# Shared experts of the second FFN in fp32r parts, dummy matmuls in TensorE's waits, and a pair of additions moved ahead of the row maximum

## The chip, the cores and the metric

The kernel runs on one core of a Trainium2 chip. Its time is the device time of one execution in microseconds; a figure for a kernel is the median of its runs. The engines are TensorE (PE in the profile, with its weight loads as PEld), VectorE (DVE), ScalarE (ACT), GpSimd (POOL) and SyncE (SP, which only issues DMAs).

## The reference

Two blocks, each an attention and a mixture of experts with gated residuals, on x of 4 x 512 x 256 in fp32 (2048 tokens):

```python
x = x + tanh(g_xattn[0]) * sliding_window_attention(layernorm(x), ctx, ctx)   # 16 heads, window 64
x = x + tanh(g_ffn[0]) * moe0(layernorm(x))      # 32 experts, 8 per token, 1 shared expert
x = x + tanh(g_xattn[1]) * coattention(layernorm(x), ctx)
x = x + tanh(g_ffn[1]) * moe1(layernorm(x))      # 8 experts, 2 per token, 2 shared ones
# coattention(enc, ctx):
Sim = (enc @ w1)[:, :, None] + (ctx @ w2)[:, None, :] + einsum('bid,bjd->bij', enc * w3, ctx) + b
hq  = softmax(Sim, axis=2) @ ctx
bar = softmax(max(Sim, axis=2), axis=1) @ enc    # one row per batch
out = concatenate([enc, hq, enc * hq, enc * bar]) @ W_qv + b_qv
# the shared experts of moe1:
z = (silu(xt @ sw1.T) * (xt @ sw3.T)) @ sw2.T    # 256 -> 512 -> 256
```

## The kernel before

Tokens lie in 16 tiles of 128 rows, four tiles to a batch (TPB = 4). The 256 columns are two halves of 128 (CH = 2). Each engine has its own instruction list, written out by hand in the order in which it is to run; semaphores tie the lists together. The program runs in these stages (microseconds of the profiled execution): the window attention, 0 to 251; `front0_tensor` with the routing of the first FFN, 256 to 343; its sparse loop over 159 blocks, 347 to 611; its shared expert and the first gathers of its result, 612 to 659; the coattention in four rounds, one for each batch, with the shared experts of the second FFN in between, 671 to 903; the rest of that FFN's routing, to 936; its sparse loop, 939 to 1081; the last shared part and the stores.

`front0_tensor` transposes the normalised rows (L767), forms the logits (L821), counts the mask's ranks (`ranks`, L787) once VectorE has chosen the experts, and builds the list of tokens by slot (`table`, L801: for each of 16 tiles eight matmuls of a one-hot `hot_tok` and a one-hot `hot_hi`, both read with a step of eight elements). `expert_row` follows, and then the sparse loop's first gather.

Stage two, round b. TensorE runs, as its list is written: `transposes(b)` (L1472), `scores(b)` (L1485), `inputs_turned(b-1)` and `logits(b-1)` of the batch before (L1558, L1569), `shared_gate_up(b-1, 0)` (L1585), `probs_transposed(b)` (L1497), `maxima_transposed` (L1503), `attended(b)` (L1520, between its halves `maximum_spread`, L1507, which waits for VectorE's `nmx`), `shared_gate_up(b-1, 1)`, `context_bar(b)` (L1529), `shared_gate_up(b-1, 2)`, half of `output(b)` (L1545), `shared_gate_up(b-1, 3)`, the other half. `shared_down(b-2)` (L1632) stands between the transposes and the scores of rounds 2 and 3, `shared_down(2)` behind round 3, and `shared_down(3)` behind the second sparse loop. A unit u of the shared experts is 128 of the 512 hidden columns: `shared_gate_up` is 2 x CH fp32 matmuls of 512 columns, ScalarE takes the silu (L1680), VectorE multiplies (`shared_hidden`, L1803, into `hid`), and `shared_down` is 4 x 4 fp32 matmuls of 256 columns. Their weights, `wsh1`, come with one DMA that SP issues in round 1.

VectorE adds the first FFN's expert rows to x in pairs of tiles (`y_pair_added`, L1193, 16 additions), two pairs for each batch; POOL gathers these rows (`yg`, L1178) as ring slots come free. In round b VectorE adds the pairs of batch b+1 and then normalises them (L720 to L751 into `xn`), which `transposes(b+1)` waits for. In round b >= 2 `shared_added(b-2)` (L1640) stands ahead of `logits_taken` (L1796).

## Time and profile before

| | us |
|---|---|
| runs | 1104.25, 1104.73, 1109.32 |
| median | 1104.73 |
| profiled execution | 1107.14 |
| its span, first to last instruction | 1105.3 |
| TensorE busy | 904.4 (82%) |
| VectorE busy | 696.2 (63%) |
| ScalarE busy | 441.5 (40%) |
| POOL busy | 538.2 (49%) |
| mean granted TensorE clock | 0.894 of full |

The shares are averages over stages that differ: in the sparse loops TensorE is busy nearly always, in routing it waits for VectorE. The granted clock takes two values, 1.0 (2.4 GHz) and 0.5 (1.2 GHz); a value between them is a mean over a stretch that has both. The same matmul lasts twice as long at 0.5.

### The profile page before, as it was taken

The numbers are of one execution on the slowest core, as the hardware profiler recorded it, in microseconds if no ns is written. First come the engines' busy times: TensorE is split into PE (matmuls) and PEld (weight loads), VectorE is DVE, ScalarE is ACT, GpSimd is POOL, SyncE is SP. The second block draws the span as 40 slices with busy tenths as digits, with TensorE's granted clock in tenths as the row PEclk, the third lists the DMA queues.
The fourth block names the chain that finished last, engine by engine and source line by source line (L and its number), as shares of the span: only waits on it lengthen the run. The fifth ranks groups of instructions, "written<-read, shape, count | busy, mean of one in ns | idle before, by whom it ended". The sixth has DMA issues, their size and how long they took to land.

```text
span 1105.3 us, 20321 instructions
## 1 busy us (share of the span) xinstructions
PE 904.4 (82%) x5372; PEld 692.5 (63%) x5373; DVE 696.2 (63%) x2004; ACT 441.5 (40%) x1030; POOL 538.2 (49%) x575
## 2 busy tenths in 40 slices
PE   3468888887297999999999904879999996998893
PEld 2357777777144888888888502545656563787672
DVE  6669999996664865555555256765868246443334
ACT  4558888992051444444444302122322313232220
POOL 7246656644004755555552577874700000687641
PEclk9679999995556999999999966969999998899997
DMA  8860000003101777777768738342300011466647
GB/s 248 212 123 3 1 0 0 0 1 107 43 1 51 220 219 202 224 215 220 214 192 138 281 95 278 105 141 80 112 6 20 1 61 23 82 111 127 139 75 243
DMA packets 75225, 127.42 MB, mean 115 GB/s; under 512 B 12481, under 2 KB 52033, under 8 KB 75009
## 3 DMA queue, kind: packets, MB, share of 16 engines
q0 software_dynamic: 21264, 48.02, 19.5%
q1 hardware_dynamic: 32240, 57.47, 17.1%
q10 hardware_dynamic: 21632, 20.85, 5.4%
q8 instruction: 44, 0.72, 0.3%
q14 instruction: 45, 0.36, 0.1%
HBM read 80.62 MB, written 36.77 MB: 106 GB/s over the span
## 4 chain that ended last, share of the span: by engine, by line
PE 60%; DVE 19%; issue 6%; DMA 6%; POOL 3%; ACT 2%; SPq 2%; DVEq 0%; ACTq 0%; POOLq 0%
PE bank L899 18%; PE bank L914 9%; PE bank L1585 5%; PE bank L888 4%; DVE ptl L609 4%; PE bank L801 3%; DMA sw<-in_w 3%; POOL yg L1178 3%; PE bank L1485 3%; DVE nmax L601 2%; PE bank L907 2%; PE bank L419 2%; DVE x L1193 2%; PE bank L1520 2%; PE bank L1632 2%
## 5 line engine op out<-in xcount | busy, mean ns | idle before, releaser
L1163 POOL DMA_INDIRECT xg<-token_rows,gather_idx x198 | 190.7, 963 | 318.3 <-DMA token_rows<-cw 135.6
L899 PE MATMUL bank<-sw,xgt 128*128 x948 | 247.5, 384 | 0.0
L899 PEld LDWEIGHTS bank<-sw,xgt 128*128 128x128 f32 x948 | 167.6, 193 | 15.2
L1178 POOL DMA_INDIRECT yg<-slot_rows,slot_of x128 | 137.0, 1070 | 70.3 <-issue 33.5
L992 ACT ACTIVATE ssil<-bank 128x128 f32<-128x128 f32 x237 | 65.7, 278 | 202.1 <-PE bank L899 202.1
L914 PE MATMUL bank<-sw,sht 128*128 x474 | 145.0, 388 | 0.0
L1084 DVE COPY xgt<-bank 128x256 f32<-128x256 f32 x198 | 83.9, 424 | 85.4 <-PE bank L888 77.3
L1097 DVE COPY sht<-bank 128x128 f32<-128x128 f32 x237 | 69.1, 291 | 106.4 <-PE bank L907 106.1
L537 ACT ACTIVATE prob<-bank,nmax 128x256 f32<-128x256 f32 x256 | 111.7, 511 | 7.5 <-DVE nmax L601 7.5
L419 PE MATMUL bank<-consts,prob 128*128 128x128 f32 x512 | 83.5, 288 | 34.7 <-DVE ptl L609 32.2
L601 DVE TENSOR_REDUCE nmax<-bank 128x2 f32<-128x512 f32 x128 | 87.6, 685 | 16.6 <-PE bank L406 15.7
L888 PE MATMUL bank<-consts,xg 128*128 128x128 f32 x396 | 78.2, 280 | 19.2 <-DMA xg<-token_rows,gather_idx 10.9
L527 ACT ACTIVATE pth<-bank 128x512 f16<-128x512 f32 x128 | 80.1, 626 | 31.9 <-PE bank L419 31.7
L419 PEld LDWEIGHTS bank<-consts,prob 128*128 128x128 f32 x512 | 57.4, 145 | 49.9 <-ACT prob L537 28.1
L609 DVE TENSOR_TENSOR ptl<-bank,pth 128x512 f16<-128x512 f32 x128 | 87.0, 680 | 1.1 <-ACT pth L527 0.8
L914 PEld LDWEIGHTS bank<-sw,sht 128*128 128x128 f32 x474 | 71.6, 191 | 19.7 <-issue 1.8
L888 PEld LDWEIGHTS bank<-consts,xg 128*128 128x128 f32 x396 | 56.0, 144 | 41.7 <-DMA xg<-token_rows,gather_idx 13.0
L1142 POOL DMA_INDIRECT token_sums<-ysb,scatter_idx x39 | 61.8, 1584 | 35.5 <-ACT ysb L999 31.8
L1007 ACT ACTIVATE ysb<-bank 128x256 f32<-128x256 f32 x159 | 61.1, 384 | 44.0 <-PE bank L914 43.5
L653 POOL TENSOR_TENSOR qm<-qst,consts 128x512 fp32r<-128x512 f32 x64 | 67.6, 1087 | 21.9 <-ACT qst L469 21.9
L406 PE MATMUL bank<-kst,qm 128*128 (+1 forms) x256 | 77.6, 386 | 0.0
L1090 DVE TENSOR_TENSOR shid<-ssil,bank 128x128 f32<-128x128 f32 x237 | 66.2, 280 | 4.7 <-ACT ssil L992 4.5
(216 smaller groups left out, 1570.5 us busy)
## 6 DMA issues: line engine op xcount, KB each, us to landing
slot_rows<-ysb ACTq DMA_DIRECT2D x79, 256.0 KB, 3.4
sw<-in_w SPq DMA_DIRECT2D x48, 384.0 KB, 3.6
kst<-khl SPq DMA_DIRECT2D x32, 224.0 KB, 5.6
token_sums<-zeros SPq DMA_DIRECT2D x2, 2176.0 KB, 12.1
token_rows<-xn SPq DMA_DIRECT2D x8, 512.0 KB, 3.6
sums<-token_sums SPq DMA_DIRECT2D x8, 512.0 KB, 7.2
xg<-token_rows,gather_idx POOLq DMA_INDIRECT x198, 3.5
x<-in_x SPq DMA_DIRECT2D x4, 512.0 KB, 6.7
```

The lines of the kernel that those rows point to most:

```text
L406: mm = pe.matmul(sp[:, hh * WIN:(hh + 1) * WIN], qm[:, par, hh, k, :], ks, start=False, stop=True, skip_group_check=True)
L419: mm = pe.transpose(bank[2 + (k + 1) % 2][:, hh * WIN + kb * P:hh * WIN + kb * P + P], prob[:, (k + 1) % 4, hh, kb * P:(kb + 1) * P], ident)
L527: nc.scalar.activation(pth[:, (k + 1) % 4], bank[2 + (k + 1) % 2][:, :].rearrange("p (a b) -> p a b", a=2), ACT.Copy).then_inc(s_pth, 1)
L537: e = nc.scalar.activation(prob[:, k % 4, hh, :], s_bank(k, par)[:, hh * WIN:(hh + 1) * WIN], ACT.Exp, bias=nmax[:, k % 4, hh:hh + 1])
L601: nc.vector.tensor_reduce(nmax[:, k % 4, :], s_bank(k, par)[:, :].rearrange("p (a b) -> p a b", a=2), AX_X, ALU.max, negate=True).then_inc ...
L609: nc.vector.tensor_tensor(ptl[:, k % 4], bank[2 + k % 2][:, :].rearrange("p (a b) -> p a b", a=2), pth[:, k % 4], ALU.subtract).then_inc(s ...
L888: mm = pe.transpose(bank[i % 2][:, c * P:(c + 1) * P], xg[:, (first + i) % XG_RING, c * P:(c + 1) * P], ident)
L899: mm = pe.matmul(bank[2 + k % 2][:, 0:2 * FF], xgt[:, i % 3, c * P:(c + 1) * P], w[:, :, c, :], start=(c == 0), stop=(c == CH - 1))
L914: pe.matmul(bank[6 + i % 2][:, 0:DIM], sht[:, k % 2, :], sw[:, bass.ds(slot[i] + u, 1), 2 * CH * FF:WCOLS], start=(u == 0), stop=(u == hal ...
L1084: nc.vector.tensor_copy(xgt[:, i % 3, :], bank[i % 2][:, 0:CH * P]).then_inc(s_xtl, 1)
L1163: nc.gpsimd.indirect_dma_start(xg[:, (first + i) % XG_RING, 0:ROW[L]], None, rows[L], bass.IndirectOffsetOnAxis(gather_idx[:, i:i + 1], 0) ...
L1178: nc.gpsimd.indirect_dma_start(yg[:, t % Y_TILES, j, :], None, ybuf[L], bass.IndirectOffsetOnAxis(slot_of[:, t, j:j + 1], 0)).then_inc(s_y ...
```

## The change

Three things change.

First, the second FFN's shared experts. Each fp32 operand is replaced by a high part, rounded to fp32r by a ScalarE copy, and a low part, the rest, by a subtract: `whi`/`wlo` for the weights (copied by ScalarE and subtracted by VectorE once, ahead of round 0), `xh`/`xl` for the inputs of each batch (`inputs_high` on ScalarE, `inputs_low` on VectorE), `hh`/`hl` for the hidden values (`hidden_high` on ScalarE; `hidden_low` on VectorE for batches 0 and 3, on POOL for 1 and 2). Each fp32 matmul becomes three fp32r ones: high x high, low x high, high x low. The raw weights now come by two DMAs (1 MB and 0.5 MB) that SP issues as soon as the first sparse loop is through, into `prob1` and `hq`, which are free there. TensorE gets waits for `wlo`, `xlo` and `hlo`.

Second, `kept_busy`: n matmuls of the identity with 256 fp32 columns of constants into a bank whose content is not used. They stand behind the window attention (4 and 5), ahead of and behind the ranks (7, 5), ahead of the table (8, behind a wait for VectorE's 21st routing step, the slots' positions), behind both `expert_row` (8, 8), ahead of the first transposes of stage two (7), behind the scores of rounds 0 and 1 (7, 5) and behind the outputs of round 0 (8).

Third, `y_pair_added(0, 4b+4)`, the first pair of the next batch, moves on VectorE from behind `negated_maximum(b)` to ahead of `shared_hidden(b-1, 0)` and `largest(b)`.

```diff
-        wsh1 = sb("wsh1", [P, SH1, WCOLS], F32)
+        whi = sb("whi", [P, SH1, WCOLS], F32R)
+        wlo = sb("wlo", [P, SH1, WCOLS], F32R)
...
+        def kept_busy(pe, to, n):
+
+            for _ in range(n):
+                pe.matmul(to[:, 0:DIM], ident, consts[:, 0:DIM], start=True, stop=True)
...
-            for k in range(5):
+            for k in range(4):
                 step(TILES, k, 0, True)
+            pe.wait_ge(s_p, UNITS)
+            kept_busy(pe, bank[4], 4)
+            step(TILES, 4, 0, True)
+            kept_busy(pe, bank[4], 5)
...
             logits(3)
+            pe.wait_ge(m.rs, 5)
+            kept_busy(pe, bank[7], 7)
             ranks(pe, 0, m)
+            kept_busy(pe, bank[7], 5)
+            pe.wait_ge(m.rs, 21)
+            kept_busy(pe, bank[7], 8)
             table(pe, 0, m, range(TILES))
             expert_row(pe, 0, m)
+            kept_busy(pe, bank[7], 8)
...
+                if L == 1 and 2 <= k < 2 + 2 * SH1 and k % 2 == 0:
+                    hidden_high(act, m, BATCH - 1, (k - 2) // 2)
...
+                if L == 1 and 6 <= k < 6 + 2 * SH1 and k % 2 == 0:
+                    hidden_low(dve, nc.vector, BATCH - 1, (k - 6) // 2)
...
                 if b == 1:
-                    sp.dma_start(wsh1[:, :, :], w1_in[0:SH1].rearrange("u p c -> p u c")).then_inc(m.wload, 16)
...
                 if v == 0:
-                    pe.wait_ge(m.wload, 16)
+                    pe.wait_ge(A["wlo"], SH1)
                 else:
                     pe.wait_ge(m.h, n1["h"] + v)
                 if u == 0:
                     pe.wait_ge(A["p"], 4 * min(b + 2, BATCH))
+                    pe.wait_ge(A["xlo"], CH * (b + 1))
                 for half, ready in ((0, m.gate), (1, m.up)):
+                    n = 0
                     for c in range(CH):
                         w = slice((CH * half + c) * FF, (CH * half + c + 1) * FF)
-                        mm = pe.matmul(bank[half][:, :], wsh1[:, u, w], xt[:, 0, c, :], start=(c == 0), stop=(c == CH - 1))
+                        for wp, xp in ((whi, xh), (whi, xl), (wlo, xh)):
+                            mm = pe.matmul(bank[half][:, :], wp[:, u, w], xp[:, c, :], start=(n == 0), stop=(n == 5))
+                            n += 1
                     mm.then_inc(ready, 1)
             pe.wait_ge(A["par"], 64)
             pe.wait_ge(A["wq"], 16)
+            pe.wait_ge(moe[0].acc, BATCH)
+            pe.wait_ge(s_yadd, 4 * TOP0 - 4)
+            kept_busy(pe, bank[7], 7)
             pe.wait_ge(A["one"], 1)
...
                 scores(b)
+                if b == 0:
+                    kept_busy(pe, bank[7], 7)
+                if b == 1:
+                    kept_busy(pe, bank[7], 5)
...
                     shared_gate_up(b - 1, 3)
                 output(b, (2,))
+                if b == 0:
+                    kept_busy(pe, bank[7], 8)
...
         def shared_down(pe, m, b):
-            pe.wait_ge(m.h, m.n["h"] + SH1 * (b + 1))
+            pe.wait_ge(A["hlo"], SH1 * (b + 1))
...
             for j in range(TPB):
+                n = 0
                 for u in range(SH1):
-                    mm = pe.matmul(bank[6 + j // 2][:, (j % 2) * DIM:(j % 2 + 1) * DIM], hid1[:, u, j * P:(j + 1) * P],
-                                   wsh1[:, u, 2 * CH * FF:WCOLS], start=(u == 0), stop=(u == SH1 - 1))
+                    for hp, wp in ((hh, whi), (hh, wlo), (hl, whi)):
+                        mm = pe.matmul(bank[6 + j // 2][:, (j % 2) * DIM:(j % 2 + 1) * DIM], hp[:, u, j * P:(j + 1) * P],
+                                       wp[:, u, 2 * CH * FF:WCOLS], start=(n == 0), stop=(n == 3 * SH1 - 1))
+                        n += 1
...
+        def hidden_high(act, m, b, u):
+            act.wait_ge(m.h, m.n["h"] + SH1 * b + u + 1)
+            nc.scalar.activation(hh[:, u, :], hid1[:, u, :], ACT.Copy).then_inc(A["hhi"], 1)
+
+        def hidden_low(eng, ops, b, u):
+            eng.wait_ge(A["hhi"], SH1 * b + u + 1)
+            ops.tensor_tensor(hl[:, u, :], hid1[:, u, :], f32(hh[:, u, :]), ALU.subtract).then_inc(A["hlo"], 1)
...
+                if b == 0:
+                    act.wait_ge(A["wlo"], SH1)
...
+            def inputs_high(b):
+                if b:
+                    act.wait_ge(m.up, m.n["up"] + SH1 * b)
+                for c in range(CH):
+                    act.wait_ge(m.xh, m.n["xh"] + 2 * b + c + 1)
+                    nc.scalar.activation(xh[:, c, :], xt[:, 0, c, :], ACT.Copy).then_inc(A["xhi"], 1)
+
+            act.wait_ge(m.wload, 32)
+            for part, source in ((gate_up_cols, prob1), (down_cols, down_raw)):
+                for u in range(0, SH1, 2):
+                    nc.scalar.activation(whi[:, u:u + 2, part], source[:, u:u + 2, :], ACT.Copy).then_inc(A["whi"], 1)
...
                 softmax(b)
                 if b:
                     inputs_copied(b - 1)
+                    inputs_high(b - 1)
                     shared_silu(b - 1, 0)
                 probs_copied(b)
                 row_exp(b)
                 attended_copied(b)
                 if b:
                     for u in range(1, SH1):
+                        hidden_high(act, m, b - 1, u - 1)
                         shared_silu(b - 1, u)
+                    hidden_high(act, m, b - 1, SH1 - 1)
...
+            def inputs_low(b):
+                for c in range(CH):
+                    dve.wait_ge(A["xhi"], CH * b + c + 1)
+                    nc.vector.tensor_tensor(xl[:, c, :], xt[:, 0, c, :], f32(xh[:, c, :]), ALU.subtract).then_inc(A["xlo"], 1)
+
             y_pair_added(dve, 0, 0)
+            n = 0
+            for part, source in ((gate_up_cols, prob1), (down_cols, down_raw)):
+                for u in range(0, SH1, 2):
+                    n += 1
+                    dve.wait_ge(A["whi"], n)
+                    nc.vector.tensor_tensor(wlo[:, u:u + 2, part], source[:, u:u + 2, :], f32(whi[:, u:u + 2, part]),
+                                            ALU.subtract).then_inc(A["wlo"], 1)
             y_pair_added(dve, 0, 2)
...
                 encoder(b)
+                if b == 2:
+                    hidden_low(dve, nc.vector, 0, 3)
                 if b:
                     residual(b - 1)
...
                 if b >= 2:
                     shared_added(dve, m, b - 2)
                 if b:
+                    inputs_low(b - 1)
                     logits_taken(b - 1)
+                if b + 1 < BATCH:
+                    y_pair_added(dve, 0, 4 * b + 4)
+                if b:
                     shared_hidden(b - 1, 0)
                 largest(b)
                 negated_maximum(b)
-                if b + 1 < BATCH:
-                    y_pair_added(dve, 0, 4 * b + 4)
+                if b == 1:
+                    hidden_low(dve, nc.vector, 0, 0)
                 products(b)
                 if b:
                     shared_hidden(b - 1, 1)
                 row_softmax(b)
                 weights_by_bar(b)
+                if b == 1:
+                    hidden_low(dve, nc.vector, 0, 1)
                 if b:
                     shared_hidden(b - 1, 2)
                 if b + 1 < BATCH:
                     y_pair_added(dve, 0, 4 * b + 6)
+                    if b == 1:
+                        hidden_low(dve, nc.vector, 0, 2)
...
             for t in range(TILES):
                 y_gathered(pool, 0, t)
+            for b in (1, 2):
+                for u in range(SH1):
+                    hidden_low(pool, nc.gpsimd, b, u)
...
             sp.wait_ge(s_sye, BLOCKS[0])
+            raw = w1_in[0:SH1].rearrange("u p c -> p u c")
+            sp.dma_start(prob1[:, :, :], raw[:, :, 0:2 * CH * FF]).then_inc(moe[1].wload, 16)
+            sp.dma_start(down_raw, raw[:, :, 2 * CH * FF:WCOLS]).then_inc(moe[1].wload, 16)
             parameters_a1(sp)
```

On VectorE in round 0, before, between the last normalised probabilities (`prob`) and the second pair; `nmx` is the row maximum, `ngmx` its spread form, `w` the weights of the context bar:

```order
L1730 TENSOR_SCALAR prob<-prob,rd 128x512
L1744 TENSOR_REDUCE nmx<-bank 1x1
L1748 COPY ngmx<-bank 128x1
L1193 SCALAR_TENSOR_TENSOR x<-yg,gate_of,x 128x256 x16
L1757 TENSOR_TENSOR prod<-enc,bank 128x512 x2
L1752 RECIPROCAL ebr<-bank 128x1
L1763 TENSOR_SCALAR hbar<-bank,ebr 128x2
L1766 SCALAR_TENSOR_TENSOR w<-wqv,hbar 128x256 x2
```

and the same stretch of the changed program, whose own line numbers these are:

```order
L1797 TENSOR_SCALAR prob<-prob,rd 128x512
L1219 SCALAR_TENSOR_TENSOR x<-yg,gate_of,x 128x256 x16
L1811 TENSOR_REDUCE nmx<-bank 1x1
L1815 COPY ngmx<-bank 128x1
L1824 TENSOR_TENSOR prod<-enc,bank 128x512 x2
L1819 RECIPROCAL ebr<-bank 128x1
L1830 TENSOR_SCALAR hbar<-bank,ebr 128x2
L1833 SCALAR_TENSOR_TENSOR w<-wqv,hbar 128x256 x2
```

The 16 additions of the pair have passed nmx and ngmx and now stand directly behind the probabilities.

On VectorE in round 2, before, from the last probabilities to the products; the L1640 rows are `shared_added(0)`, `lg` is `logits_taken(1)`, `hid` is `shared_hidden(1, 0)`:

```order
L1730 TENSOR_SCALAR prob<-prob,rd 128x512
L1640 SCALAR_TENSOR_TENSOR x<-bank,tg,x 128x256 x4
L1796 COPY lg<-bank 128x32
L1803 TENSOR_TENSOR hid<-hid,bank 128x512
L1744 TENSOR_REDUCE nmx<-bank 1x1
L1748 COPY ngmx<-bank 128x1
L1193 SCALAR_TENSOR_TENSOR x<-yg,gate_of,x 128x256 x16
```

and of the changed program:

```order
L1797 TENSOR_SCALAR prob<-prob,rd 128x512
L1681 SCALAR_TENSOR_TENSOR x<-bank,tg,x 128x256 x4
L1875 TENSOR_TENSOR xl<-xt,xh 128x512 x2
L1863 COPY lg<-bank 128x32
L1219 SCALAR_TENSOR_TENSOR x<-yg,gate_of,x 128x256 x16
L1870 TENSOR_TENSOR hid<-hid,bank 128x512
L1811 TENSOR_REDUCE nmx<-bank 1x1
L1815 COPY ngmx<-bank 128x1
```

The two subtracts for xl, which gate_up(1, 0) waits for, have come in behind `shared_added`, and the pair has moved up as in round 0.

On TensorE of the changed program, from the first transposes of stage two (L1496) to the first shared matmul (L1612); left out are the matmuls between the probabilities and the outputs, which are as before:

```order
L392 MATMUL bank<-consts 128x256 x7
L1496 MATMUL bank<-consts,xn 128x128 x8
L1509 MATMUL bank<-craw,aenc 128x512 x8
L392 MATMUL bank<-consts 128x256 x7
L1521 MATMUL bank<-consts,prob 128x128 x16
...
L392 MATMUL bank<-consts 128x256 x8
L1496 MATMUL bank<-consts,xn 128x128 x8
L1509 MATMUL bank<-craw,aenc 128x512 x8
L392 MATMUL bank<-consts 128x256 x5
L1582 MATMUL bank<-consts,xn 128x128 x8
L1593 MATMUL bank<-rraw,xt 128x8 x8
L1612 MATMUL bank<-xh,whi 128x512
```

Before, the rows of L392 are not there; the others follow one another in this order.

## Rows read from the trace of the kernel before

**Rows 1.** The page: the chain that ended last, by engine.
```profile
PE 60%; DVE 19%; issue 6%; DMA 6%; POOL 3%; ACT 2%; SPq 2%; DVEq 0%; ACTq 0%; POOLq 0%
```

**Rows 2.** Windows of TensorE: stretch, length, busy (instructions), granted clock, DMA share, GB/s.
```profile
258.65:279.05 20.40, 20.37 (x96) 0.50 0.52 163
291.90:295.50 3.60, 3.54 (x31) 0.62 0.00 0
305.70:342.70 37.00, 36.94 (x129) 0.50 0.00 1
347.40:354.40 7.00, 5.06 (x16) 0.62 0.41 112
674.90:684.90 10.00, 9.95 (x16) 0.73 1.05 382
...
722.40:732.50 10.10, 10.02 (x16) 0.72 0.36 104
743.30:749.50 6.20, 6.20 (x11) 0.57 0.25 73
```

**Rows 3.** Timeline of TensorE: start, length, operation, shape, count, idle before.
```profile
244.16 0.38 PE L403 MATMUL bank<-band,identb 128*128 128x512 bf16 x1
244.18 0.58 PE L406 MATMUL bank<-kst,qm 128*128 128x256 f32 x2
...
773.30 3.60 PE L1585 MATMUL bank<-xt,wsh 128*128 128x512 f32 x8
...
783.19 7.17 PE L1632 MATMUL bank<-wsh,hid 128*128 128x256 f32 x32 [0.24 <-DVE hid L1803]
...
800.02 1.95 PE L1569 MATMUL bank<-rraw,xt 128*128 128x8 f32 x16 [1.70 <-ACT xt L1674]
```

**Rows 4.** Groups by line and shape: busy us, mean ns, idle before.
```profile
L653 POOL TENSOR_TENSOR qm<-qst,consts 128x512 fp32r<-128x512 f32 x64 | 67.6, 1087 | 21.9 <-ACT qst L469 21.9
...
L1302 DVE TENSOR_TENSOR same<-same,cw 128x512 f32<-128x512 f32 x8 | 5.5, 684 | 0.0
...
L481 ACT ACTIVATE khl<-kraw 128x1792 fp32r<-128x1792 f32 x2 | 3.4, 1698 | 9.7 <-DMA kst<-khl 9.7
```

**Rows 5.** The chain that ended last, at the first sparse loop's end.
```profile
612.28 2.16 DMA slot_rows<-ysb
```

**Rows 6.** The page: DMA issues, count, KB each, median us to landing.
```profile
slot_rows<-ysb ACTq DMA_DIRECT2D x79, 256.0 KB, 3.4
```

**Rows 7.** Timeline of POOL and VectorE at the first two pairs.
```profile
645.68 2.86 POOL L1178 DMA_INDIRECT yg<-slot_rows,slot_of  x1 [0.30 <-issue]
...
640.91 6.82 DVE L1193 SCALAR_TENSOR_TENSOR x<-yg,gate_of,x 128x256 f32<-128x256 f32 x17
659.14 1.27 DVE L1193 SCALAR_TENSOR_TENSOR x<-yg,gate_of,x 128x256 f32<-128x256 f32 x3 [11.41 <-DMA yg<-slot_rows,slot_of]
```

**Rows 8.** The chain that ended last, at the first FFN's table.
```profile
305.76 36.93 PE bank L801 x128
```

**Rows 9.** Timeline of TensorE at the second FFN's table.
```profile
926.62 1.02 PE L1585 MATMUL bank<-xt,wsh 128*128 128x512 f32 x2
927.48 0.87 PE L801 MATMUL bank<-hot_hi,hot_tok 128*128 128x39 f16 x8
```

**Rows 10.** Timeline of VectorE and TensorE in round 0.
```profile
693.49 0.28 DVE L1744 TENSOR_REDUCE nmx<-bank 1x1 f32<-1x128 f32 x1 [4.08 <-PE bank L1503]
...
705.72 0.88 DVE L1766 SCALAR_TENSOR_TENSOR w<-wqv,hbar 128x256 f32<-128x256 f32 x2
...
701.13 1.93 PE L1529 MATMUL bank<-eb,xn 128*128 128x1 f32 x16
```

**Rows 11.** Timeline of ScalarE and VectorE in round 2.
```profile
798.89 1.07 ACT L1674 ACTIVATE xt<-bank 128x512 f32<-128x512 f32 x2
...
801.92 1.65 DVE L1640 SCALAR_TENSOR_TENSOR x<-bank,tg,x 128x256 f32<-128x256 f32 x4
...
838.09 0.68 DVE L1803 TENSOR_TENSOR hid<-hid,bank 128x512 f32<-128x512 f32 x1
```

More of the change, by code:

```diff
@@ L134, in gated_xattn_moe_kernel @@
         wsh0 = sb("wsh0", [P, WCOLS], F32)
-        wsh1 = sb("wsh1", [P, SH1, WCOLS], F32)
+        whi = sb("whi", [P, SH1, WCOLS], F32R)
+        wlo = sb("wlo", [P, SH1, WCOLS], F32R)
+        xh = sb("xh", [P, CH, SEQ], F32R)
+        xl = sb("xl", [P, CH, SEQ], F32R)
         hid1 = sb("hid1", [P, SH1, SEQ], F32)
+        hl = sb("hl", [P, SH1, SEQ], F32R)
+        hh = sb("hh", [P, SH1, SEQ], F32R)
         lg1 = sb("lg1", [P, TILES, E1], F32)
@@ L201, in gated_xattn_moe_kernel @@
         hq = sb("hq", [P, CH, SEQ], F32, a1)
+        down_raw = hq[:, :, :].rearrange("p c (a f) -> p (c a) f", f=DIM)
+        gate_up_cols, down_cols = slice(0, 2 * CH * FF), slice(2 * CH * FF, WCOLS)
         prod = sb("prod", [P, CH, SEQ], F32, a1)
@@ L330, in gated_xattn_moe_kernel @@
             "msim", "mx", "mxt", "nmx", "gmx", "ngmx", "eb", "ebr", "hb", "hbc", "w14", "hq", "hqh", "prod", "o", "x",
-            "one", "bg", "bx")}
+            "one", "bg", "bx", "whi", "wlo", "xhi", "xlo", "hhi", "hlo")}
         s_out = sem("out_stored")
@@ L1441, in sync_a1 @@
                 if b == 1:
-                    sp.dma_start(wsh1[:, :, :], w1_in[0:SH1].rearrange("u p c -> p u c")).then_inc(m.wload, 16)
-                if b == 1:
                     sp.wait_ge(s_zero, 1)
@@ L1622, in tensor_a1 @@
             expert_row(pe, 1, m)
+            kept_busy(pe, bank[7], 8)
         def shared_down(pe, m, b):
-            pe.wait_ge(m.h, m.n["h"] + SH1 * (b + 1))
+            pe.wait_ge(A["hlo"], SH1 * (b + 1))
             if b == BATCH - 1:
@@ L1692, in scalar_a1 @@
                     for u in range(1, SH1):
+                        hidden_high(act, m, b - 1, u - 1)
                         shared_silu(b - 1, u)
+                    hidden_high(act, m, b - 1, SH1 - 1)
             b = BATCH - 1
             inputs_copied(b)
+            inputs_high(b)
             act.wait_ge(m.rs, 2)
@@ L1864, in vector_a1 @@
             shared_added(dve, m, b - 1)
+            inputs_low(b)
             logits_taken(b)
```

## The prediction

> **What bounds the kernel now.** I read the chain of waits first: three fifths of it are TensorE, a fifth VectorE [rows 1]. TensorE is thus the engine to watch, but only where it neither waits nor is slowed. The windows view then gives TensorE's granted clock for the stretches where that chain stays on it outside the sparse loops [rows 2]. In each of them the reader is to see a busy time close to the length of the stretch and a clock of 0.50 to 0.73, that is a stretch lying wholly or partly at the lower of the two levels. Busy time multiplied by the clock is what the same work would take at full speed: 10.02 x 0.72 = 7.2 us for the scores of round 1. What the engine did before the clock fell is the same each time: it waited for VectorE or a transfer. [...] Third come prices of operations, by shape [rows 3, 4], and last the timeline of the places where the change adds a wait [rows 7, 10, 11].
>
> **The change part by part.** I sum along the profiled execution, 1107.14 us with a span of 1105.3; it lies 2.4 above the median of the three runs, 1104.73, so what I find is subtracted from the median.
>
> *Price of the parts.* An fp32 shared_gate_up is 3.60 us for 4 matmuls of 512 columns; shared_down is 7.17 for 16 of 256 [rows 3]. An fp32r matmul of 512 columns does not occur. The nearest rows are bf16 with 512 columns, ending at 244.54, and behind it two fp32r of 256 columns, ending at 244.76: 0.11 each, thus 0.22 for 512. Twelve of them make 2.6, which is 1.0 less than fp32, in each of 16 units. The 48 in shared_down would be 5.3; but each has a weight load, and 16 matmuls of 8 columns, where only the load counts, took 1.95, 0.12 each [rows 3], which gives 5.9. I take 5.7, a gain of 1.5 for each of four.
>
> *Up to the first sparse loop: -3.4.* The matmuls behind attention's end sit at 0.50 because of what they are; nine dummies before them may hold the clock for a moment: -0.9 (nothing to -10, half of 20.4). Seven dummies before the ranks lie in TensorE's wait for VectorE's selection; if the clock is up behind them, 3.54 x 0.38 = -1.3. The eight behind expert_row fill the wait for the first gather: the window there has 5.06 busy at 0.62, so up to -1.9, of which I take -1.2, since gathers end some of its waits. The table itself, 36.93 us at 0.50, I leave as it is: 128 matmuls of 159 columns are 0.288 each, and at full clock eight of 39 columns took 0.87 less 0.16 of the matmul ahead, about 0.09 [rows 8, 9]. Both fit a fixed 0.02 and 1.66 ns for each column whatever the clock; the operands are strided. The other reading is the second rival.
>
> *Start of stage two: +2.6 -1.5.* VectorE now makes wlo between its first and second pair. Two subtracts of 1024 and two of 512 columns at 684 ns per 512 [rows 4] are 4.1 us. They fit in its own idle time of 11.41 before the second pair; what is late is POOL, whose gathers end that wait. While the first pair ran, 6.82 us, gathers took up to 2.86 where 0.95 is usual [rows 7]; the excess of those in the stretch is 2.4, so 4.1 us cost +1.4. The raw load of 1.5 MB is issued just ahead of the last slot_rows store, which releases POOL: it landed in 2.16 where 3.4 is the median with loads about [rows 5, 6], +1.2. Bounds: nothing, and 4.1 + 1.2 = +5.3 if POOL stands still through each subtract. The Trainium skill has a rule for it (SBUF — State Buffer, "SBUF: two separate sides"): a VectorE instruction with two SBUF inputs locks out a GpSimd one that reads SBUF for the whole instruction. The trace agrees in part, since gathers stretched by 2.4 of 6.8 us; by the rule the term would be the upper bound and the sum 2.7 later. Seven dummies before the first transposes can lift the scores of round 0 from 0.73 to full, 9.95 x 0.27 = 2.7; the pauses for enc and aenc may undo it, so I take half: -1.5.
>
> *Round 0, the pair: -3.2.* Before, VectorE idles 4.08 us ahead of nmx and has the 16 additions of a pair behind ngmx. TensorE ended the context bar at 703.06, but VectorE came to w at 705.72 [rows 10]. With the pair moved into that idle time w follows TensorE, -2.7, and TensorE's transposes of probabilities, at full clock after seven dummies, give about 0.5. nmx becomes late in turn, behind 6.4 us of pair, and TensorE waits about 1 for it at maximum_spread; that is included, since otherwise its gain would be nearer 1.5.
>
> *Round 1: -6.4.* Eight dummies bridge the wait for xn: the transposes gain 1.0, and of the scores' 2.8 [rows 2] 2.5 lie ahead of VectorE's next chain. Then inputs_low stands behind the last probability, and gate_up(0,0) starts 0.2 earlier where TensorE alone would have given 1.6. It took 6.2 at 0.57; as parts it is 2.6 at full clock or 5.2 at half; the middle gives -2.2. Two later units give -1.9; two hidden_low subtracts on VectorE cost +1.4 ahead of xn(2).
>
> *Start of round 2: +3.5.* A new chain: VectorE's hid(0,3), ScalarE's hh (0.6), only then its encoder(2) (1.1, two copies as at 798.89 [rows 11]), VectorE's aenc (1.4, two of 684 ns) and behind it hl (0.7). Queued behind hl is shared_down(0), and behind that the scores. That is 3.8, where TensorE waited 0.24 [rows 3]; the 1.5 that shared_down gains I give away again for a start at half clock.
>
> *Rounds 2 and 3: +1.9 and -1.5.* In round 2 xt is copied at 799.96, xh needs 1.2 more, and xl stands behind shared_added, whose last of four ends at 803.57 [rows 11]; with 1.4 for xl gate_up(1,0) starts at 804.95, not 801.83: +3.1, and +0.9 for its clock. Four units give -3.8. hl(1,3) is on POOL, 1.1 [rows 4], behind hid at 838.77 [rows 11] and hh 0.6: +2.2 with the semaphores until shared_down(1), whose own -1.5 shrinks to -0.5 by its clock: +1.9. In round 3 +3.1, -3.8 and -1.5, since POOL has hl ready in time there, and +0.7 for the clock: -1.5.
>
> *Tail and second loop: -3.0 and -2.0.* Four units -3.8, xl +0.8 where VectorE has little ahead of it. In the second loop: clock at its start as in the first, -1.2; four pairs of subtract and copy among VectorE's and ScalarE's work +0.7, hidden if TensorE bounds there; the last shared_down -1.5.
>
> Sum: -3.4 +2.6 -1.5 -3.2 -6.4 +3.5 +1.9 -1.5 -3.0 -2.0 = **-13.0**, so 1094.1 for such an execution and **1092** for the median.
>
> **The rivals.** *The clock is not held.* Dummies end before what they are for, with idle time behind them: after scores(1) TensorE waits for VectorE's chain, before the table for the rest of the slots. Then 0.9, 1.3, 1.2 and 1.2 at the loops' sides, 1.5 and 3.5 + 2.2 in rounds 0 and 1 are lost, 11.8 in all: 1104. For it speaks that 20 us of busy time at 0.50 did not raise the clock [rows 2].
>
> *The table follows the clock.* Its rows also fit a load of 128 and 159 columns one after the other, 287 in 0.288 us at half and 167 in 0.09 at full, twice as fast. If the clock is up when it starts and stays up, 287 in 0.155 makes 19.8 for the 128, and some 2 more for one-hots that come tile by tile: -15, so 1077. Against it stands the same pause ahead of the table.
>
> *The new waits are worse.* Each of xl, hl on VectorE and hl on POOL leaves TensorE idle 3 to 4.5 us; if every gate_up(b,0) and shared_down behind one runs wholly at half clock, that is 1.7 and 4 more than summed, in three rounds and two: about +10, 1102.
>
> *Slower: fp32r at fp32's half rate.* It decides where 12 matmuls cost the 3.54 of the four, at 0.295 us for 512 columns. At 0.43 the 16 units lose 1.6 each against fp32, not gain 1.0, and each shared_down 3.1 instead of gaining 1.5: 42 + 18 = 60 more: about 1150. The row that is against it has 256 columns and only two matmuls, with modelled ends [rows 3].
>
> **How the numbers follow.** My forecast 0.53, its own range 1085 to 1099; clock not held 0.12; table 0.18; waits 0.12; fp32r slow 0.05. About 0.5%, 5.5 us, is what a measurement of this kernel tells from no change. Faster: 0.18 and nearly all of the forecast, 0.70. Same: the two cases at 1102 to 1104 for the most part, 0.22. Slower: fp32r and a loss of both clock and waits, 0.08. The range runs from the table's 1077 to 1104.
>
> **What would show it.** In the changed profile: units of about 2.6 us and shared_down of 5.7; a clock above 0.9 in the ranks and in the scores of round 1; the table still 37 us; TensorE waiting some 3 us for xl before gate_up(1,0), and over 4 for hl before shared_down(0); wlo beside slower gathers, with the second pair ending later by 2 to 3. A table of 22, units above 3.5, or clocks of 0.5 in the named stretches would make the prediction wrong.

## The result and the profile after

The changed kernel is slower: a median of 1115.1 us (1111.8 to 1118.15, nine runs) against 1104.73 in runs beside it, a ratio of 1.0086 with a 95% interval of 1.0062 to 1.0111. The forecast was 1092, from 1077 to 1104. The profiled execution took 1115.51 with a span of 1113.7, 8.4 longer than the span of before (the medians differ by 10.4); its mean granted clock rose from 0.894 to 0.901. The clock is thus better and the time worse, and the question is which stages gave back what the clock brought.

The page after, busy time of each engine and the granted clock in 40 slices:

```profile
PE 929.0 (83%) x5644; PEld 739.6 (66%) x5645; DVE 711.7 (64%) x2024; ACT 457.1 (41%) x1058; POOL 553.8 (50%) x583
PEclk9779999997757999999999958979888897999997
```

I compare the two traces at landmarks of TensorE's list. A step's error is what its stretch added, less what the prediction gave it:

| landmark | shift against before | its step | predicted | error |
|---|---|---|---|---|
| last result of the first sparse loop | -2.0 | -2.0 | -3.4 | +1.4 |
| transposes of round 0 (674.88) | +3.6 | +5.6 | +2.6 | +3.0 |
| transposes of round 1 (721.38) | +2.5 | -1.1 | -4.7 | +3.6 |
| transposes of round 2 (781.19) | -0.7 | -3.2 | -6.4 | +3.2 |
| scores of round 2 (794.13) | +3.9 | +4.6 | +3.5 | +1.1 |
| scores of round 3 (858.00) | +12.2 | +8.3 | +1.9 | +6.4 |
| inputs turned behind round 3 (914.35) | +12.3 | +0.1 | -1.5 | +1.6 |
| end | +8.4 | -3.9 | -5.0 | +1.1 |

The errors add up to 21.4, from -13.0 to +8.4. No single step carries them; round 2 has the most. The first row and the last hold scatter. Ahead of the first dummy, near the end of the window attention, TensorE is already 1.35 later than before (252.18 against 250.83). `pair_only` and `parts_only`, two kernels of the section below, have the program of before up to there and lie 2.65 apart at its last matmul (252.41 and 255.06). Counted from there the first row is -3.3, as predicted. For the last row see the end of the account below.

Windows of TensorE after, in the columns of [rows 2]:

```profile
292.30:294.20 1.90, 1.86 (x24) 1.00 0.00 0
305.00:309.40 4.40, 4.40 (x16) 1.00 0.02 4
310.00:341.00 31.00, 31.00 (x110) 0.50 0.00 0
...
678.40:688.70 10.30, 8.97 (x17) 0.85 1.03 377
724.30:734.10 9.80, 9.77 (x17) 0.74 0.34 102
...
786.30:794.30 8.00, 7.95 (x49) 0.72 0.36 103
...
808.60:814.10 5.50, 5.46 (x13) 0.50 0.01 3
849.40:858.10 8.70, 8.67 (x49) 0.64 0.00 0
```

The first rows are the ranks, now at full clock (busy 1.9, before 3.5), and two stretches of the first table: 16 matmuls in 4.40 at full clock, 110 in 31.0 at half, both about 0.28 each. The other five are where the forecast hoped for clock or feared for it: scores of round 0 at 0.85 (before 0.73), scores of round 1 no better than before, `shared_down(0)` at 0.72, `gate_up(1,0)` wholly at half, `shared_down(1)` at 0.64.

### The profile page after: what moved, and what is told of

It reads as the page before. It is cut to its first block and busy times, and to the rows that moved or that the text cites. A ratio compares the mean times of both kernels' runs of the same rounds, so it can differ in the third digit from the quotient of the medians.

```text
span 1113.7 us, 20927 instructions
## 1 busy us (share of the span) xinstructions
PE 929.0 (83%) x5644; PEld 739.6 (66%) x5645; DVE 711.7 (64%) x2024; ACT 457.1 (41%) x1058; POOL 553.8 (50%) x583
## 5 line engine op out<-in xcount | busy, mean ns | idle before, releaser
L1204 POOL DMA_INDIRECT yg<-slot_rows,slot_of x128 | 141.9, 1109 | 62.1 <-issue 34.1
L392 PE MATMUL bank<-consts 128*128 128x256 f32 x144 | 43.5, 466 | 38.4 <-DVE x L1219 30.1
## 6 DMA issues: line engine op xcount, KB each, us to landing
token_sums<-zeros SPq DMA_DIRECT2D x2, 2176.0 KB, 12.2
```

The lines of the kernel that those rows point to most:

```text
L1204: nc.gpsimd.indirect_dma_start(yg[:, t % Y_TILES, j, :], None, ybuf[L], bass.IndirectOffsetOnAxis(slot_of[:, t, j:j + 1], 0)).then_inc(s_y ...
```

## The experiments

Theory: the dummies do what they were meant to, and the fp32r parts cost more than they save, by their waits and at the start of stage two. Rivals: the dummies are what costs time; the moved pair is. The ratios below are each to runs of the kernel before on the same chip; 0.1% is 1.1 us.

**The three parts of the change, one at a time.** `pair_only` is before with only the pair moved:

```diff
+                if b + 1 < BATCH:
+                    y_pair_added(dve, 0, 4 * b + 4)
                 if b:
                     shared_hidden(b - 1, 0)
...
                 negated_maximum(b)
-                if b + 1 < BATCH:
-                    y_pair_added(dve, 0, 4 * b + 4)
```

> The kernel before with the moved pair alone. Theory A (the fp32r parts and the waits and transfers they bring lose the time; pair and dummies gain a little): 1 to 4 us under before, since w in round 0 no longer stands behind the pair. Theory B (the dummies, or the moved pair through a late row maximum, lose the time): equal to before or up to 3 us over it.

Measured: 1.0013 (0.9989 to 1.0038), nothing. VectorE in round 0, timeline; the answer to [rows 10]:

```profile
688.32 6.42 DVE L1193 SCALAR_TENSOR_TENSOR x<-yg,gate_of,x 128x256 f32<-128x256 f32 x16
...
702.77 0.88 DVE L1766 SCALAR_TENSOR_TENSOR w<-wqv,hbar 128x256 f32<-128x256 f32 x2
...
704.80 6.04 DVE L1193 SCALAR_TENSOR_TENSOR x<-yg,gate_of,x 128x256 f32<-128x256 f32 x15 [0.75 <-DMA yg<-slot_rows,slot_of]
```

The weights w do come earlier, but the second pair now comes too early for POOL's gathers and waits for them, and the transposes of the next round wait for that pair as they did.

`dummies_only` is before with every `kept_busy` of the change and its waits, and nothing else; `parts_only` is the changed kernel without the dummies and with the pair at its old place. One place of the many, as it stands in the first and as it is taken out of the second:

```diff
 # dummies_only against before
                 scores(b)
+                if b == 0:
+                    kept_busy(pe, bank[7], 7)
...
 # parts_only against the changed kernel
                 scores(b)
-                if b == 0:
-                    kept_busy(pe, bank[7], 7)
...
```

> The kernel before with the dummy matmuls alone. Theory A: 2 to 5 us under before, of which 2 by the end of the first sparse loop, as in the changed kernel's trace; table at 0.288 us a matmul at either clock. Theory B: over before by several us, since eight dummies at half clock run for 6 us and stand ahead of the first gathered rows.

> The changed kernel without the dummies and with the pair at its old place, thus the fp32r parts alone. Theory A: 12 to 18 us over before: some 5 at the start of stage two (slot rows' store and POOL's gathers), the rest in rounds 2 and 3. Theory B: within 3 us of before.

Measured: dummies 0.9907 (0.988 to 0.9933), parts 1.0164 (1.0137 to 1.0191). That decides between the theory and its rivals: the dummies alone save 10 us, twice the most that was expected, and the parts alone cost 18. TensorE's windows with dummies alone:

```profile
347.00:353.00 6.00, 4.12 (x22) 1.00 0.37 106
...
716.40:723.70 7.30, 7.30 (x17) 1.00 0.33 102
```

The first gather's window and the scores of round 1 are at full clock, 7.3 for the latter, where the changed kernel with the same dummies needs 9.8.

`dummies_and_pair` and `parts_and_dummies` complete the square, the first being `dummies_only` with the pair moved, the second the changed kernel with the pair moved back (the diff of `pair_only`, forwards and backwards).

> The kernel before with dummies and moved pair, without the fp32r parts. Theory A: 4 to 9 us under before, the sum of the two alone or a little more, since the pair gives TensorE less time to idle. Theory B: over before.

> The changed kernel with the pair back at its old place. Dummies alone were at 0.991 of before and dummies with the pair at 0.9975, so the pair cost there. Theory A (the pair's 16 additions come earlier, but the second pair then waits for POOL's gathers and nmx is late, so it brings nothing and, with the clock up, loses): 1.002 to 1.007 of before, under the changed kernel's 1.0086, and w about 1.5 later in round 0 with no wait of the second pair for a gather. Theory B (the pair pays beside the parts): 1.010 to 1.015.

Measured: 0.9975 (0.9955 to 0.9995) and 1.0079 (1.0051 to 1.0107), the first a smaller gain and the second a higher time than theory A expected. With the parts in, the pair is again nothing: 1.0079 against 1.0086. The parts cost as much on top of the dummies (0.9907 to 1.0079, 1.7%) as alone (1.6%). One reading does not fit: beside the dummies alone the pair costs 0.7%, and the intervals do not touch. The one execution of that kernel that was traced took 1177.76, far from the kernel's median of 1101.78, and shows no place for it; this stays open.

**What the parts cost.** `raw_late` lets SP issue the raw weights only when the last slot_rows stores have landed; the parameter loads behind them in SP's list wait with them:

```diff
             sp.wait_ge(s_sye, BLOCKS[0])
+            for r in range(Y_RING):
+                sp.wait_ge(s_yst[r], 64 + 16 * len(range(r, PFIRST[0] + PAIRED[0], Y_RING)))
```

> The changed kernel with the two raw weight loads issued only when the last slot rows have landed. Theory A (the loads hold up the last store, which releases POOL): the first gather about 2 us earlier against the first loop's end, and 2 us under the changed kernel's 1115. Theory B (the pause has another cause): no gain, or slower, since the weights and parameters come later.

`wlo_late` moves the four subtracts for wlo on VectorE from between the first two pairs to behind `encoder(0)`:

```diff
             y_pair_added(dve, 0, 0)
-            n = 0
-            for part, source in ((gate_up_cols, prob1), (down_cols, down_raw)):
...
             y_pair_added(dve, 0, 2)
...
                 encoder(b)
+                if b == 0:
+                    n = 0
+                    for part, source in ((gate_up_cols, prob1), (down_cols, down_raw)):
...
```

> The changed kernel with the four subtracts for wlo behind the first encoder scaling, where VectorE waits for the scores of round 0. Theory A (POOL stands still while VectorE runs these subtracts): no gather of 6 us, the second pair 3.5 us earlier, 3 to 4 us under the changed kernel, unless gathers for the third pair now come late. Theory B (gathers are only somewhat slower beside VectorE): 1 us under it.

Measured: 1.0064 (1.004 to 1.0087) and 1.0056 (1.0034 to 1.0077), 2.4 and 3.3 us off the changed kernel's 1.0086. Each interval overlaps that of the changed kernel, so the sizes rest on the traces. Here is the changed kernel at the start of stage two, POOL and VectorE; the answer to [rows 5, 7]:

```profile
615.30 0.94 POOL L1204 DMA_INDIRECT yg<-slot_rows,slot_of  x1 [23.38 <-DMA slot_rows<-ysb]
...
643.32 6.34 POOL L1204 DMA_INDIRECT yg<-slot_rows,slot_of  x1 [0.31 <-issue]
...
638.94 6.42 DVE L1219 SCALAR_TENSOR_TENSOR x<-yg,gate_of,x 128x256 f32<-128x256 f32 x16
645.28 2.35 DVE L1883 TENSOR_TENSOR wlo<-prob,whi 128x1024 fp32r<-128x1024 f32 x2
647.55 1.28 DVE L1883 TENSOR_TENSOR wlo<-hq,whi 128x512 fp32r<-128x512 f32 x2
```

One gather stands from 643.32 to 649.66, until 0.8 after wlo's last subtract; the longest of before at the first two pairs was 2.86. In `raw_late` the first gather, and in `wlo_late` the gather in the first pair (639.97 to 646.4) and those beside wlo at its new place:

```profile
612.27 0.94 POOL L1204 DMA_INDIRECT yg<-slot_rows,slot_of  x1 [20.82 <-DMA slot_rows<-ysb]
```

```profile
643.95 3.26 POOL L1204 DMA_INDIRECT yg<-slot_rows,slot_of  x1 [0.30 <-issue]
...
677.47 1.43 POOL L1204 DMA_INDIRECT yg<-slot_rows,slot_of  x1 [0.30 <-issue]
...
675.13 2.35 DVE L1897 TENSOR_TENSOR wlo<-prob,whi 128x1024 fp32r<-128x1024 f32 x2
677.40 1.29 DVE L1897 TENSOR_TENSOR wlo<-hq,whi 128x512 fp32r<-128x512 f32 x2
```

With SP's loads held back the last store releases POOL 2.45 after the loop's last result (609.82), not 5.02; before, with the parameter loads beside the store but not the raw weights, it was 2.92. Without wlo behind the pair the stuck gather is 3.26 again, and wlo alone, 3.6 us of VectorE, stretches a gather to no more than 1.43.

`no_low_parts` is the changed kernel without the subtracts for xl and hl; the high part is multiplied in their place, so that TensorE's work keeps its size:

```diff
-                        for wp, xp in ((whi, xh), (whi, xl), (wlo, xh)):
+                        for wp, xp in ((whi, xh), (whi, xh), (wlo, xh)):
...
-            pe.wait_ge(A["hlo"], SH1 * (b + 1))
+            pe.wait_ge(A["hhi"], SH1 * (b + 1))
```

> The changed kernel with the low parts of inputs and hidden values left out: xl and hl are never made, the high part stands in their place in the matmuls, which stay as many. Theory A (the loss of rounds 2 and 3 is in the waits for xl and hl and in the clock that falls in them): 10 to 14 us under the changed kernel, with shared_down(0) and (1) under 7 us. Theory B (the fp32r matmuls themselves, or ScalarE's copies, cost it): under 4 us gained.

Measured: 0.9962 (0.9944 to 0.998), 13.7 us off. TensorE at `shared_down(0)`:

```profile
782.93 0.39 PE L1670 MATMUL bank<-whi,hh 128*128 128x256 f32 x1 [1.42 <-ACT hh L1685]
```

The wait is 1.42 instead of 4.07, and the 48 matmuls take 6.0. This kernel takes the subtracts off VectorE and POOL as well as the waits off TensorE, so the price is that of both. The three prices, 13.7 + 2.4 + 3.3 = 19.4, come close to what separates the changed kernel from the dummies alone (1.0086 less 0.9907, 19.8). That is a sum over three runs with one price gone in each; no run has all three gone. If it holds, the fp32r parts are worth nothing to speak of even then, though their matmuls are cheaper; the account of the steps below says where that went.

**Is it the length of the new waits or the clock behind them?** `waits_filled` puts more dummies into the new waits of the changed kernel: 8 and 5 ahead of `shared_down(0)` and `(1)`, 6, 3 and 3 behind the turned inputs, 3 and 5 ahead of `gate_up(1,0)` and `(2,0)`:

```diff
+                    kept_busy(pe, bank[7], (8, 5)[b - 2])
...
+                    pe.wait_ge(A["x"], 4 * b)
+                    kept_busy(pe, bank[4], (6, 3, 3)[b - 1])
...
+                    if b >= 2:
+                        kept_busy(pe, bank[2], (3, 5)[b - 2])
```

> The changed kernel with more dummies in TensorE's new waits: ahead of shared_down(0) and (1) (8, 5), behind inputs_turned(b-1) (6, 3, 3) and ahead of gate_up(1,0) and (2,0) (3, 5). Theory A1 (the waits cost mostly by the clock that falls in them): gate_up(b,0) and shared_down at full clock, 6 to 10 us under the changed kernel. Theory A2 (the waits cost by their own length): within 3 us of it.

Measured: 1.0025 (0.9992 to 1.0057). Windows of TensorE, the two `shared_down` and `gate_up(1,0)`:

```profile
784.10:790.10 6.00, 5.96 (x49) 1.00 0.37 109
...
804.60:807.60 3.00, 3.00 (x14) 1.00 0.00 0
842.60:848.60 6.00, 6.00 (x49) 1.00 0.00 0
```

All at full clock, while TensorE still waits for VectorE's xl. From scores(2) to scores(3) it is 55.6 before, 63.9 after and 58.4 here: of the 8.3 the clock makes 5.5. The 2.8 that are left are the waits by their length, still 5.7 in this kernel (2.9 for xl, 2.8 for hl), less 2.9 that the cheaper matmuls give back. So in this round the clock and the length cost about the same.

`parts_mended` joins `raw_late`, `wlo_late` and `waits_filled`, with the pair at its old place:

> The changed kernel with all three mends together (raw weights after the last slot rows, wlo behind the first encoder scaling, TensorE's new waits filled) and the pair back at its old place. Theory A (start of stage two 5.5, clock in the new waits some 6, pair nothing): 1100 to 1104, at or a little under before, and still 5 to 9 over the kernel with the dummies alone, since the waits for xl and hl keep their length. Theory B (the fp32r parts pay once those costs are gone): under the 1095.6 of the dummies alone.

Measured: 1.0002 (0.9972 to 1.0032). The parts, mended where the runs pointed, are level with before. But this kernel has the dummies too. Against fp32 with dummies, `dummies_filled` below, measured beside it at 0.9908, it is still 10 us slower. Of the 13.7 that `no_low_parts` took off, filling the waits took 6.7; the other 7, for the waits' length and the subtracts, fit most of these 10, and the rest stays open.

**A faster version.** `dummies_filled` is `dummies_only` with the dummies of `waits_filled` behind the turned inputs (6, 3, 3). `dummies_filled_tail` has three and four in the tail too; these are shown:

```diff
+            pe.wait_ge(A["x"], 4 * BATCH)
+            kept_busy(pe, bank[4], 3)
...
+            kept_busy(pe, bank[2], 4)
```

> The kernel before in fp32 with the dummies of the change and six, three and three more behind inputs_turned(0), (1) and (2); no parts, no moved pair. Theory A (the clock is worth most where TensorE bounds the round): logits and gate_up(b,0) at full clock, 3 to 6 us under the 1095.6 of the dummies alone. Theory B (fp32 units do not suffer there): no gain.

> The same with dummies in the tail as well: three behind inputs_turned(3), four ahead of gate_up(3,3). Theory A: gate_up(3,0) and (3,3) 1.7 us shorter each, of which the routing chain between them hides one: 1 to 3 us under the kernel without them. Theory B: no gain, since VectorE's routing ends last there.

Measured: 0.9908 (0.9877 to 0.9939), no better than `dummies_only`, and 0.9877 (0.9829 to 0.9926), 1090.61 us. Three windows of the latter, `gate_up(2,0)`, `gate_up(3,0)` and `gate_up(3,3)`:

```profile
842.80:848.20 5.40, 5.40 (x12) 0.68 0.01 2
891.20:894.90 3.70, 3.70 (x10) 1.00 0.37 107
906.60:910.30 3.70, 3.70 (x11) 1.00 0.00 0
```

`dummies_only` has 5.4 in all three. Here `gate_up(2,0)`, behind three dummies and a wait of 0.40 for xt, still takes 5.4; `gate_up(3,0)`, behind three dummies and no wait, takes 3.7, and so does `gate_up(3,3)` behind four. It is the fastest of all, but its interval overlaps that of `dummies_only`.

## Why the prediction was wrong, step by step

**The price of the parts: right by the matmul, wrong for the unit.** TensorE after, in a unit of round 1, and then the first matmul of the later three units of round 2 and of the next transposes; below them the same four places with fp32, from `dummies_only`:

```profile
764.56 0.48 PE L1612 MATMUL bank<-xh,whi 128*128 128x512 f32 x1
...
767.14 0.39 PE L1612 MATMUL bank<-xh,wlo 128*128 128x512 f32 x1
767.37 1.89 PE L1569 MATMUL bank<-wqv,hq 128*128 128x256 f32 x8
...
823.64 0.80 PE L1612 MATMUL bank<-xh,whi 128*128 128x512 f32 x1
...
828.75 0.48 PE L1612 MATMUL bank<-xh,whi 128*128 128x512 f32 x1
...
836.56 0.58 PE L1612 MATMUL bank<-xh,whi 128*128 128x512 f32 x1
...
845.57 1.09 PE L1496 MATMUL bank<-consts,xn 128*128 128x128 f32 x8 [0.74 <-DVE xn L767]
```

```profile
806.88 3.60 PE L1600 MATMUL bank<-xt,wsh 128*128 128x512 f32 x8
810.31 0.28 PE L1541 MATMUL bank<-ebs,ones 128*128 128x1 f32 x2
...
812.24 3.68 PE L1600 MATMUL bank<-xt,wsh 128*128 128x512 f32 x8
...
820.93 3.60 PE L1600 MATMUL bank<-xt,wsh 128*128 128x512 f32 x8
...
829.55 1.04 PE L1487 MATMUL bank<-consts,xn 128*128 128x128 f32 x8
```

Twelve starts from 764.56 on are about 0.23 apart, and the next matmul starts 2.81 behind the first: the price of 2.6 was nearly right, and fp32r at half rate is excluded. But the 3.60 that it was set against reaches past the start of the next matmul: from start to start an fp32 unit takes 3.43 (806.88 to 810.31), so a unit gains 0.6. Over 16 units that is some 6 us less than forecast, by this estimate. From start to start the three later units of round 2 with what follows them take 21.93, with fp32 22.67. So "1.0 less than fp32, in each of 16 units" is the step that failed most widely: 0.7 for three units, with the 0.74 in it that TensorE now waits for xn. In round 3 `gate_up(2,0)` and the three behind it gave 3.0 of 3.8, and the wait for xl took 3.0 as predicted; a wait of 0.96 for xn behind `shared_down(2)` took what that had gained. In the tail it was +0.3 where -3.0 stood: `gate_up(3,0)` and `(3,3)` run at half clock, where twelve matmuls of 0.427 take 5.1, little less than the 5.4 of before. `shared_down` takes 6.0 at full clock (48 of 0.12 to 0.125), against the 5.7 taken.

**Round 2, the largest error.** ScalarE, VectorE and TensorE after, ahead of `shared_down(0)` and ahead of `gate_up(1,0)`, and POOL ahead of `shared_down(1)`; the answer to [rows 11]:

```profile
783.02 0.63 ACT L1687 ACTIVATE hh<-hid 128x512 fp32r<-128x512 f32 x1 [8.29 <-DVE hid L1870]
783.56 1.07 ACT L1697 ACTIVATE enc<-bank 128x512 f32<-128x512 f32 x2
784.17 1.53 DVE L1785 TENSOR_SCALAR aenc<-bank,wsim 128x512 f32<-128x512 f32 x2 [1.18 <-ACT enc L1697]
785.62 0.68 DVE L1691 TENSOR_TENSOR hl<-hid,hh 128x512 fp32r<-128x512 f32 x1
786.35 0.58 PE L1672 MATMUL bank<-whi,hh 128*128 128x256 f32 x1 [4.07 <-DVE hl L1691]
...
802.82 1.07 ACT L1725 ACTIVATE xt<-bank 128x512 f32<-128x512 f32 x2
803.78 1.16 ACT L1738 ACTIVATE xh<-xt 128x512 fp32r<-128x512 f32 x2
805.64 1.65 DVE L1681 SCALAR_TENSOR_TENSOR x<-bank,tg,x 128x256 f32<-128x256 f32 x4
807.21 1.28 DVE L1875 TENSOR_TENSOR xl<-xt,xh 128x512 fp32r<-128x512 f32 x2
808.64 0.76 PE L1612 MATMUL bank<-xh,whi 128*128 128x512 f32 x1 [1.53 <-DVE xl L1875]
...
848.12 1.26 POOL L1691 TENSOR_TENSOR hl<-hid,hh 128x512 fp32r<-128x512 f32 x1 [13.35 <-ACT hh L1687]
849.43 0.58 PE L1672 MATMUL bank<-whi,hh 128*128 128x256 f32 x1 [2.77 <-POOL hl L1691]
```

The chains are the predicted ones, instruction by instruction, and their lengths fit: hid, hh, enc, aenc, hl make TensorE wait 4.07 (3.8 predicted); xl costs `gate_up(1,0)` 2.9 (3.1); hl on POOL 2.8 (2.2). What stands behind them does not. `gate_up(1,0)` runs wholly at half clock, +1.7 where 0.9 stood; `shared_down(1)` starts at half, 1.6 longer than before where 0.5 shorter was summed; and the units give 0.7 back, not 3.8. With hl and xl these make 0.8 + 2.1 + 3.1 + 0.6 - 0.2, the 6.4 of the table. The rival "the new waits are worse" had the mechanism and nearly the amount: it put +10 on such losses, and `waits_filled` took back 6.7.

**Start of stage two: the upper bound, not the value.** +5.6 came where 2.6 were summed and 5.3 was the bound. The late store is 2.1 of it (5.02 behind the last result, before 2.92), the stuck gather 6.34 less 2.86, 3.5. The step that failed is "4.1 us cost +1.4": a stretched share of the first pair was carried over to wlo as if every microsecond of VectorE cost the same. The Trainium skill's rule (SBUF — State Buffer, "SBUF: two separate sides"), that a VectorE instruction with two SBUF inputs, if it starts first, locks a GpSimd one that reads SBUF out for the whole instruction, would have given the bound. The traces agree with it for the end of a long stretch only: there one gather stood 6.34, but the three ahead of it beside the same stretch took 0.95 to 1.22.

**Rounds 0 and 1.** In round 0 -1.1 came of -4.7. The scores ran at 0.85 instead of 0.73, but a new wait of 1.29 for ScalarE's probabilities (684.95) took that gain. "With the pair moved into that idle time w follows TensorE" came true: w starts 0.5 later than in [rows 10], in a round that starts 3.6 later. Still little was gained, since the step stopped at w. TensorE's next wait is for xn, behind the second pair, and that waits for POOL's gathers. TensorE and VectorE after:

```profile
684.95 3.70 PE L1509 MATMUL bank<-craw,aenc 128*128 128x512 f32 x8 [1.29 <-ACT prob L1704]
...
706.26 0.88 DVE L1833 SCALAR_TENSOR_TENSOR w<-wqv,hbar 128x256 f32<-128x256 f32 x2
...
709.36 6.02 DVE L1219 SCALAR_TENSOR_TENSOR x<-yg,gate_of,x 128x256 f32<-128x256 f32 x15 [1.83 <-DMA yg<-slot_rows,slot_of]
```

In round 1 the transposes gained 0.6 (1.0 predicted); the scores gained nothing: 9.8 at 0.74, where -2.5 stood. `gate_up(0,0)` up to the next unit gave -1.5 (-2.2), the later units, with a wait of 0.55 for xn behind them, -1.0 (-1.9 for the units and +1.4 for hl ahead of xn). The dummies can do it, since `dummies_only` has 7.3; there TensorE waits 1.25 for xn, here 1.77. What keeps the clock down there with the parts in is not shown.

**Up to the first loop, and the rivals.** Counted from attention's end this step gave -3.3 of -3.4, the ranks right. But its -0.9 rested on the matmuls behind attention being at half clock "because of what they are", and no run shows that. In `parts_only`, which has no dummies there, the same 96 take 16.47 at a mean clock of 0.66, where before they take 20.37 at 0.50 [rows 2]:

```profile
258.00:280.00 22.00, 16.47 (x96) 0.66 0.47 152
```

So what came of that term cannot be put down to the dummies either. That the table follows the clock is disproved by the windows above. "The clock is not held" holds in part: not in round 1 with the parts in, but the dummies alone save 0.9%. The chance for slower, 0.08, was set on fp32r's rate and on a loss of both clock and waits; the second is near what came, with units that gain less, and its prices stood in the rows of before.

Behind the tail -4.2 came where -2.0 was predicted, and that is luck. All of it lies between `expert_row` and `shared_down(3)`: 143.56 us, before 147.73. This stretch scatters, for `waits_filled`, whose program is the same there, needs 147.82. From the start of `shared_down(3)` to the end it is 23.42, before 23.49: that this `shared_down` takes 5.98 instead of 7.15 gains nothing, since VectorE's last additions wait for the transfer of the sums.

## What to carry to other kernels

Price a replaced instruction from the start of the first to the start of what follows it, in the place where it stands: a busy time that reaches past the next start promises a gain that the next instruction already had. A split into high and low parts puts a copy and a subtract on two other engines ahead of every use; where the operand is the last thing to arrive, those are on the path, and the idle time that they make lets the clock fall for the work behind. Test the parts of a change one by one: here ten saved microseconds were buried under eighteen lost ones.

## What the runs showed of the hardware

VectorE's additions do not stop a POOL gather at once. Beside a continuous stretch of VectorE's additions or subtracts the early gathers pass with about 1 us, and a later one stands until 0.8 us behind the stretch (0.4 in `dummies_only`): 3.26 in one of 6.4 us, 6.34 in one of 9.9 us. Beside wlo alone, 3.6 us, none took more than 1.43.

The table's matmuls, with operands read in steps, take 0.28 us at both clock levels, while fp32r matmuls of 512 columns start 0.23 apart at full clock and 0.43 apart at half. Whether the steps are the reason no run shows. The sentence ahead of the prediction that the same matmul lasts twice as long at 0.5 has this exception.

A load of 1.5 MB, issued by SP from the moment that ScalarE issued a store of 128 KB (both at 610.31), kept that store's waiter for 5.02 us behind the last result. Before, without this load, it was 2.92, and with SP's other loads held back too 2.45.
